# VectorE's 32x32 turns with the channel outermost, and matmuls that write their banks with a stride of 32

## The reference, cut to what matters

```
x_ft = rfft2(x)                                  # x: batch, 32 channels, 64, 64
out_ft[:, :, :12, :12]  = einsum('bixy,ioxy->boxy', x_ft[:, :, :12, :12],  w1)
out_ft[:, :, -12:, :12] = einsum('bixy,ioxy->boxy', x_ft[:, :, -12:, :12], w2)
x1 = irfft2(out_ft)
x2 = einsum('bchw,oc->bohw', h, conv_w) + conv_b
h  = gelu(layer_norm(x1 + x2))                   # over the 32 channels
```

## Time and profile before

| | |
|---|---|
| runs | 5870.03, 5879.43, 5875.86 us |
| profiled execution | 5870.29 us |
| its span | 5868.6 us |
| mean granted clock of TensorE | 0.957 |
| PE, busy | 5338.6 us (91%) |
| DVE, busy | 4244.8 us (72%) |
| ACT, busy | 3689.6 us (63%) |
| POOL, busy | 1169.3 us (20%) |

### The profile page before, as it was taken

The page is one execution under the profiler, slowest core; times in us unless marked ns, Lnnn a source line. Parts: engine busy times, 40 slices in busy tenths (PEclk is TensorE's granted clock), DMA queues, the critical chain, the costliest instruction groups (busy, mean ns, idle before and its releaser), DMA issues.

```text
span 5868.6 us, 134909 instructions
## 1 busy us (share of the span) xinstructions
PE 5338.6 (91%) x43556; PEld 3021.4 (51%) x43556; DVE 4244.8 (72%) x7712; ACT 3689.6 (63%) x6005; POOL 1169.3 (20%) x1291
## 2 busy tenths in 40 slices
PE   5777789999999999999999999999999999878778
PEld 2444456666666666666666663333333333344343
DVE  5888789999898999899999884555555555444553
ACT  5777666667666677666677656567777777623333
POOL 0266300366200366200467100000000000000000
PEclk9998899999999999999999999999999999968898
DMA  1333467666777666777666772221111111000000
GB/s 66 115 124 120 139 170 225 206 213 210 215 215 218 202 213 214 215 211 226 211 212 211 215 196 66 62 63 51 51 51 51 51 52 51 20 1 7 7 7 4
DMA packets 427386, 756.21 MB, mean 129 GB/s; under 512 B 277809, under 2 KB 335922, under 8 KB 361530
## 3 DMA queue, kind: packets, MB, share of 16 engines
q1 hardware_dynamic: 410682, 714.26, 39.5%
q0 software_dynamic: 16384, 37.78, 2.2%
HBM read 397.49 MB, written 354.42 MB: 128 GB/s over the span
## 4 chain that ended last, share of the span: by engine, by line
PE 77%; DVE 10%; issue 6%; ACT 4%; SPq 1%; POOL 1%; DMA 1%; DVEq 0%; ACTq 0%; POOLq 0%
PE ps_y L892 17%; PE ps_t L904 9%; PE ps_y L885 9%; PE ps_t L991 8%; PE ps_t L913 7%; PE ps_f L926 4%; PE ps_f L976 4%; PE ps_s L939 2%; PE ps_f L961 2%; PE ps_s L871 2%; PE ps_t L1000 2%; PE ps_t L328 2%; PE ps_y L861 2%; DVE big L1254 1%; PE ps_f L318 1%
## 5 line engine op out<-in xcount | busy, mean ns | idle before, releaser
L1117 ACT ACTIVATE big<-ps_y 128x512 f32<-128x512 f32 x1280 | 773.9, 605 | 859.9 <-PE ps_y L892 784.8
L892 PEld LDWEIGHTS ps_y<-conv_now,big 128*128 128x128 f32 x8192 | 993.2, 191 | 520.2 <-issue 520.2
L1261 DVE TENSOR_REDUCE big<-big 128x16 f32<-128x512 f32 x1280 | 845.4, 678 | 531.6 <-ACT big L1117 531.3
L892 PE MATMUL ps_y<-conv_now,big 128*128 128x128 f32 x8192 | 1147.2, 283 | 0.0
L1254 DVE TENSOR_TENSOR big<-big 128x512 f32<-128x512 f32 x1280 | 878.4, 706 | 108.7 <-PE ps_t L904 102.5
L1126 ACT ACTIVATE big<-ps_t 128x512 f32<-128x512 f32 x1024 | 616.6, 602 | 474.0 <-PE ps_t L913 468.3
L904 PE MATMUL ps_t<-ident,big 128*128 128x128 f32 x5120 | 804.4, 281 | 88.5 <-DVE big L1254 86.5
L1133 ACT ACTIVATE big<-ps_t,g_now 128x512 f32<-128x512 f32 x1024 | 802.4, 784 | 63.1 <-PE ps_t L904 62.1
L1121 ACT ACTIVATE big<-ps_y 128x512 f32<-128x512 f32 x1280 | 776.1, 606 | 0.0
L904 PEld LDWEIGHTS ps_t<-ident,big 128*128 128x128 f32 x5120 | 596.3, 143 | 317.0 <-issue 207.2
L913 PE MATMUL ps_t<-ident,big 128*128 128x128 f32 x4096 | 662.0, 285 | 40.2 <-ACT big L1126 40.2
(11 more groups left out here) (179 smaller groups left out, 6775.9 us busy)
## 6 DMA issues: line engine op xcount, KB each, us to landing
hstore<-big SPq DMA_DIRECT2D x256, 1024.0 KB, 4.5
big<-hstore SPq DMA_DIRECT2D x256, 1024.0 KB, 5.1
xmodes<-x_out SPq DMA_DIRECT2D x128, 312.0 KB, 5.0
y_kt<-ymodes SPq DMA_DIRECT2D x512, 78.0 KB
ymodes<-y_st SPq DMA_DIRECT2D x192, 144.0 KB, 3.0
mix_room<-xmodes SPq DMA_DIRECT2D x64, 336.0 KB, 7.4
mix_room<-xmodes SPq DMA_DIRECT2D x64, 288.0 KB, 6.2
ymodes<-y_st SPq DMA_DIRECT2D x64, 192.0 KB, 3.3
```

Of the source, the lines that this page charges most:

```text
L892: last = mm(ps_y[:, wh, 128 * b:128 * b + 128], h_in[k // 2][:, at:at + 128], conv_now[:, :], start=False, stop=(b == 3))
L1117: af(y_sq[wh], ps_y[:, wh, :], ACT.Square).then_inc(s["sq_done"], 1)
L1261: v_.tensor_reduce(ss[:, k // 2, at:at + 16], groups(y_sq[wh]), AX.X, ALU.add).then_inc(s["ss_done"], 1)
```

## The change

VectorE's two wide turns write their output in the order in which they produce it: the 32 elements of a block's row stand side by side, and the channel is the outermost index. They still read the banks with a stride of 32. The matmuls behind them take the same columns in the order channel outermost: `inv_h` reads, for each of 32 channels, a run of 16 elements, and `fwd_w` a run of 13, the next channel 32 elements further on. So that the result lies in the banks as it did, they write with a stride of 32 elements inside the run and 1 from channel to channel. Number, order and place of the instructions on every engine are the same as before; only these three lines' patterns differ, and `turn_modes` is not touched.

```
--- before.py
+++ after.py
@@ -882,8 +882,8 @@
                 for image in range(2):
                     for wh in range(2):
                         r, half = slice(64 * image + 32 * wh, 64 * image + 32 * wh + 32), image ^ odd
-                        mm(ps_y[64 * half:64 * half + 64, wh, :], c_inh[r, :], z_kx[j][r, 512 * odd:512 * odd + 512],
-                           start=True, stop=False)
+                        mm(ps_y[64 * half:64 * half + 64, wh, :].rearrange("p (w o) -> p o w", o=32), c_inh[r, :],
+                           z_kx[j][r, :].rearrange("p (o w) -> p o w", w=32)[:, :, 16 * odd:16 * odd + 16], start=True, stop=False)
 
             def conv(k, wh):
 
@@ -936,7 +936,8 @@
                     for j in range(2):
                         for image in range(2):
                             r, at = slice(64 * image, 64 * image + 64), 64 * j + 32 * image
-                            last = mm(ps_s[at:at + 32, sx, 0:RUN], c_fww[r, :], t_w[r, j, 512 * sx:512 * sx + RUN],
+                            last = mm(ps_s[at:at + 32, sx, 0:RUN].rearrange("p (k c) -> p c k", c=32), c_fww[r, :],
+                                      t_w[r, j, :].rearrange("p (c k) -> p c k", k=32)[:, :, 16 * sx:16 * sx + KX],
                                       start=True, stop=True)
                 last.then_inc(s["fw_done"], 1)
 
@@ -1232,13 +1233,13 @@
                 i = n - QUADS
                 wait(dve, "iw_done", 2 * i + j + 1)
                 dve.wait_ge(s["y_done"], 8 * (n - 1) + 4 * j + 4)
-                v_.transpose(z_kx[j].rearrange("p (w o) -> p o w", o=32), flat(of).rearrange("p (k o) -> p o k", o=32)
+                v_.transpose(z_kx[j].rearrange("p (o w) -> p o w", w=32), flat(of).rearrange("p (k o) -> p o k", o=32)
                              ).then_inc(s["iw_read"], 1)
 
             def turn_w(m, j):
                 wait(dve, "f_done", 2 * m + j + 1)
                 wait(dve, "fw_done", m)
-                v_.transpose(t_w[:, j, :].rearrange("p (k c) -> p c k", c=32), flat(ps_f).rearrange("p (w c) -> p c w", c=32)
+                v_.transpose(t_w[:, j, :].rearrange("p (c k) -> p c k", k=32), flat(ps_f).rearrange("p (w c) -> p c w", c=32)
                              ).then_inc(s["tw_done"], 1)
 
             def turn_modes(m):
```

## The result

The changed kernel takes 5825.99 us (median of 4 runs, 5820.57 to 5830.92) against 5873.6 us of the kernel before: ratio 0.9924, 95% interval [0.9912, 0.9936]. A second set on another occasion gave 5830.5 against 5865.3 us, ratio 0.9935 [0.9918, 0.9952]. So the change is worth 35 to 48 us; the forecast was 43 (5833 us).

What follows compares the result with a forecast made beforehand. TensorE was taken to bound layers and head, with it and VectorE handing work to each other in the stem. Savings 25 + 6 + 12 = 43 us, matmuls 0, gave 5833 us at the runs' median level; range 5798 to 6030.

Steps and rivals of the forecast that it cites:

- The turn, 0.73 us: VectorE's turns L1235 and L1241: adjacent writes save 0.73 us each, from a possible 0 to 0.73; 374 us of VectorE time.
- The matmuls, 0: TensorE's inv_h (L885) and fwd_w (L939): strided bank writes and reads in runs of 16 and 13 cost 0.
- Half the pace: f32 matmuls write a bank at 0.81 ns per column, while it accepts one per 0.43 ns, so the stride is free.
- Stem, 25 + 6: Stem: 25 us less from L904's waits for normalization L1254, 6 us from mode products L961 waiting for turn L1241.
- Layers, 12: Layers: 12 us less from the 38 waits of L904 for L1254, 16.5 us in all.
- Head, 0: Head: no gain, as no wait of TensorE names the turns L1235; it waits for the copy L1303.
- Rival 1: L885 and L939 slowed by strided bank writes: 598 us at full doubling, about 6440 us in total; chance 0.29.
- Rival 2: Turns L1235 and L1241: the penalty is the bank read's and stays, 3 or 4 us saved, 5872 us; chance 0.21.
- Rival 3: Stem: turn faster, but ScalarE's L1133 and L1126 end last; 10 us remain, 5866 us; within the forecast's own 0.50.

Runs made afterwards that it cites:

- read_side: Changed kernel with L1235's turn reading and writing adjacent elements, L1241's reading adjacent and writing with a stride of 32: turns 1239 and 1989 ns, kernel 5857.5 us.
- mm_single_words: Kernel before, turns unchanged, L885 and L939 reading single words 32 elements apart and writing banks with a stride of 32: 6458.4 us, ratio 1.0995.

## Why the prediction was right, step by step

- **The turn, 0.73 us.** Right: 1985 to 1226 ns and 1992 to 1239 ns are 0.76 and 0.75. The choice of the write's side was made by an argument about the bank's pace, and the experiment read_side shows it.
- **The matmuls, 0.** Right but for the 3 to 4 us of L939, and the reason held on the bank's side with some luck. The pace of 0.43 ns per column was that of adjacent words; the pair of bf16 runs puts a separate word at about 0.85 ns, next to the f32 matmuls' 0.81. "Half the pace" made it look as if there were a reserve, and by these figures an f32 column has none left. On the reading side the sentence that runs of 13 and 16 cost nothing held, but I had thought single words free too, and they cost 584 us.
- **Stem, 25 + 6.** The sum is nearly right (some 34 us by the marks), and in part by luck. The mechanism, TensorE's waits for VectorE, gave less: its idle time fell by 19 us, where 31 was forecast. The waits of L904 fell by 20 us and not by the 25 to 32 forecast, the mode products' by 8 (6 forecast), and those for ScalarE's L1133, which I had put down as next to be late, by 9. The other 12.5 us are the same matmuls in less busy time, at a granted clock of 0.93 for 0.91, and the forecast has no term for that.
- **Layers, 12.** Too large, it was 8 (2649.5 to 2641.4), although the waits in question fell by 12.1 us (16.5 to 4.4). A wait of a weight load for VectorE isn't all time of the chain. The 4 us too many here and the 3 too few in the stem cancel in the total.
- **Head, 0.** Right: with all 61 turns of the head 0.7 us shorter it takes 1551.6 us as before, and 1548.8 the second time; kernels with the old turn there show 1548.6 as well.
- **Rival 1**, slower matmuls, did not come about; its price was sound, as mm_single_words shows, where a column at about double time cost 584 us for the 598 worked out. **Rival 2**, the read's side, is out by read_side. **Rival 3** was the low end; ScalarE did not take the turn's place, and the waits for it fell too.

## What to carry to other kernels

VectorE's time is worth what waits behind it: the same 0.75 us off 256 turns gave some 40 us where 60 of them lie in the stem, and nothing measurable where all lie in stages that TensorE fills. When a layout has to be strided somewhere, put the stride in the bank, on the read of VectorE's turn and on the write of f32 matmuls, and keep runs of adjacent words on the turn's write to SBUF and on the matmul's read from it; a stride of 32 elements is what was tried. A gain in waits can bring another in TensorE's granted clock, so compare its busy time for the same records too. After a turn gets cheap, look again at its place in the engine's order: behind the normalizations or between them, that gave another 28 us, in the quads where no mode product waits for it, and lost 25 to 31 us when it was done in all.

## What the runs showed of the hardware

- VectorE's 32x32 turn: 1239 to 1250 ns for 128x1024 with an adjacent write, whether the bank is read adjacent or with a stride of 32 elements; 1985 to 1992 ns with a write to SBUF with a stride of 32.
- An f32 matmul that reads single words from SBUF, 32 elements apart, and writes its bank with the same stride takes 1.68 ns per column (L885; L939 1.79), with runs of 16 words 0.81. At runs of 13, each followed by a hop, a record of 416 columns is 5 ns longer than with adjacent ones (514 for 509).
- Writing separate words 32 elements apart into a bank, at about 0.85 ns each by estimate, costs the f32 matmul nothing (587 ns for 512 columns as before) and takes the bf16 one from 385 to 603 ns.
- In the stem the same 5640 records of TensorE took 638 us of busy time at a granted clock of 0.91, and 626 us at 0.93.
- The stage after the head took 794.6 and 804.4 us in two executions of one and the same program, so a difference of 10 us in it says nothing of a change elsewhere.
